# The merge stage of an attention plus mixture-of-experts layer: denser head storage, a two-tile projection with a bias row, and routing in five parts

## The reference

```
x = layernorm(x + (softmax(q k^T / 4 + gate * relative_bias) v) Wo^T + bo)
logits = x Wr^T ; probs = softmax(logits) ; best two of 8 experts, capacity 2560 rows each, in token order
token that overflows any expert -> a shared fallback net instead
x = layernorm(x + sum of expert outputs by weight)
```

## Time and profile before

| | us |
|---|---|
| median of 3 runs (lowest, highest) | 3783.45 (3782.28, 3784.93) |
| the profiled execution's own time | 3788.6 |
| its span | 3786.7 |
| `merge` in it, from its first transfer to the last scatter's issue | 2386.1 to 2675.9 |
| TensorE busy over the span | 3360.6 (89%) |
| mean granted TensorE clock | 0.94 |

### The profile page before, as it was taken

The page is one execution under the profiler, slowest core; times in us unless marked ns, Lnnn a source line. Parts: engine busy times, 40 slices in busy tenths (PEclk is TensorE's granted clock), DMA queues, the critical chain, the costliest instruction groups (busy, mean ns, idle before and its releaser), DMA issues. The chain is left out here.

```text
span 3786.7 us, 61590 instructions
## 1 busy us (share of the span) xinstructions
PE 3360.6 (89%) x20980; PEld 2171.0 (57%) x20980; DVE 2150.9 (57%) x5133; ACT 2131.6 (56%) x4135; POOL 1305.1 (34%) x1788
## 2 busy tenths in 40 slices
PE   7994998989999999999999898685599999999992
PEld 4552444444444444444444443574588888888882
DVE  5765887878787878787778786376011111111115
ACT  4553887878787878787878787111222232232231
POOL 3333433333333333333333332037323223222221
PEclk9997999999999999999999999896799999999996
DMA  6666233343434333333343432663465565665666
GB/s 196 218 223 145 52 67 75 66 81 67 78 67 76 68 80 69 79 66 75 75 78 64 75 66 49 176 205 137 161 204 191 190 205 188 193 204 186 196 196 202
DMA packets 281897, 481.68 MB, mean 127 GB/s; under 512 B 59906, under 2 KB 166020, under 8 KB 263170
## 3 DMA queue, kind: packets, MB, share of 16 engines
q1 hardware_dynamic: 243970, 425.27, 42.1%
q0 software_dynamic: 26880, 35.87, 4.5%
q10 hardware_dynamic: 10752, 16.78, 1.2%
HBM read 323.47 MB, written 153.89 MB: 126 GB/s over the span
## 5 line engine op out<-in xcount | busy, mean ns | idle before, releaser
L745 DVE CUSTOM_DVE_ANT_0 tot<-sc,gbias 128x1024 f32<-128x1024 f32 x1024 | 1238.8, 1210 | 34.1 <-PE sc L645 19.8
L612 POOL TENSOR_SCALAR gbias<-slab_a,gs 128x484 f32<-128x484 f32 x1024 | 679.7, 667 | 1099.2 <-DVE negm L745 826.1
L797 ACT ACTIVATE probs<-tot,negm 128x640 f32<-128x640 f32 (+2 forms) x1024 | 766.0, 748 | 83.9 <-DVE negm L745 81.7
L645 PE MATMUL sc<-ks,qs 120*128 120x512 bf16 x2048 | 638.5, 394 | 181.7 <-DMA gs<-gate_d 153.2
L1305 ACT ACTIVATE f_hid<-f_ph,f_w_up 128x256 f32<-128x256 f32 x576 | 272.7, 473 | 722.4 <-PE f_ph L1266 722.4
L806 ACT ACTIVATE far_t<-fb 128x512 f32<-128x512 f32 (+1 forms) x1024 | 580.2, 567 | 124.2 <-PE fb L682 116.7
L757 DVE COPY near_t<-pb 128x256 f32<-128x256 f32 (+1 forms) x1024 | 397.5, 388 | 373.2 <-PE pb L666 366.1
L816 ACT ACTIVATE near_t<-pa 128x256 f32<-128x256 f32 (+1 forms) x1024 | 447.8, 437 | 209.7 <-PE pa L657 197.0
L1266 PE MATMUL f_ph<-f_xt,f_w_up 128*128 128x256 f32 x2304 | 511.9, 380 | 5.7 <-DMA f_w_up<-in_w_up 5.0
L1278 PE MATMUL f_py<-f_w_down,f_hid 128*128 128x256 f32 x2304 | 509.0, 379 | 0.0
L657 PEld LDWEIGHTS pa<-ident,probs 128*128 128x128 f32 x2560 | 335.5, 144 | 253.5 <-issue 111.9
(11 more groups left out here) (164 smaller groups left out, 3092.9 us busy)
## 6 DMA issues: line engine op xcount, KB each, us to landing
f_w_down<-in_w_down SPq DMA_DIRECT2D x72, 1152.0 KB, 5.3
f_w_up<-in_w_up SPq DMA_DIRECT2D x72, 1028.0 KB, 7.7
xg_d<-fill SPq DMA_DIRECT2D x113, 260.0 KB, 5.2
ks<-k_d SPq DMA_DIRECT2D x192, 128.0 KB
qs<-q_d SPq DMA_DIRECT2D x192, 128.0 KB
f_xin<-xg_d SPq DMA_DIRECT2D x72, 260.0 KB, 5.2
v_d<-vt SPq DMA_DIRECT2D x16, 1024.0 KB, 6.2
vs<-v_d SPq DMA_DIRECT2D x32, 512.0 KB, 11.8
```

The source lines that it names most:

```text
L612: pool.tensor_scalar(gbias[x % NG][:, SIDE:SIDE + BAND], slab[:, hh, :], gs[u % 2][:, i, hh:hh + 1], 1.0, ALU.mult, ALU.mult).then_inc(gbi ...
L645: mm = pe.matmul(sc[:, x % 2, c * 512:(c + 1) * 512], qs[u % 2][0:120, hh, i * P:(i + 1) * P], ks[u % 2][0:120, hh, c * 512:(c + 1) * 512] ...
L745: dve.tensor_tensor_reduce(tot[x % 2][:], sc[:, x % 2, :], gbias[x % NG][:, w:w + N], -1.0, 3.0e38, ALU.add, ALU.min, negm[h % 2][:, c:c + ...
L797: act.activation(probs[x % 2][:, 0:hi - lo], tot[x % 2][:, lo:hi], ACT.Exp, bias=negm[h % 2][:, c:c + 1], scale=-1.0).then_inc(near_done, 1)
```

## The change

Six edits, all but the first in `merge`:

1. `ot_d` has two groups of 128 full rows in place of four of 128 with padding; `store` issues four transfers of 16 rows each, and the waits count 64 for each half.
2. `project_out` is one product of a row of ones with `b_o`, then two of 128 rows; `w_o` and `b_o` come in one transfer each, and POOL clears nothing but sets `eps`.
3. `load` moves half as many bytes of attention output.
4. The constants count on a semaphore of their own, `consts_in`, for which TensorE and VectorE wait at iteration 6; the second load is queued ahead of them.
5. The token numbers are loaded as a tile of 128 by 64 and copied to `x1s` by one VectorE instruction.
6. The parts are 15, 14, 13, 11 and 11 tiles, so routing begins at iterations 22, 36, 49, 60 and 71.

```diff
-    ot_d = dram("ot_d", [HQ, B, P, N], F32)
+    ot_d = dram("ot_d", [EC, B, P, N], F32)
...
-                    sp.wait_ge(ot_stored, h * 16)
+                    sp.wait_ge(ot_stored, h * 64)
...
-                sp.dma_start(ot_d[g, b, :, s * 512:(s + 1) * 512], rcb[:]).then_inc(ot_stored, 16)
+                for hh in range(4):
+                    row = (g % 2 * 4 + hh) * D
+                    sp.dma_start(ot_d[g // 2, b, row:row + D, s * 512:(s + 1) * 512], rcb[32 * hh:32 * hh + D, :]).then_inc(ot_stored, 16)
...
-PARTS = (20, 18, 15, 11)
+PARTS = (15, 14, 13, 11, 11)
...
-        w_o = sb("w_o", [P, HQ, E])
+        w_o = sb("w_o", [P, EC, E])
+        b_o = sb("b_o", [1, E])
-        otl = sb("otl", [P, NB, HQ, TC * P])
+        otl = sb("otl", [P, NB, EC, TC * P])
...
-            sp.wait_ge(w_zero, 1)
-            for h in range(4):
-                sp.dma_start(w_o[32 * h:32 * h + D], a["wo"].rearrange("(g h d) n -> h d g n", h=4, d=D)[h]).then_inc(loaded, 16)
-
-            sp.dma_start(w_o[D:D + 1, 0, :], a["bo"]).then_inc(loaded, 16)
+            sp.dma_start(w_o[:], a["wo"].rearrange("(c p) n -> p c n", p=P)).then_inc(loaded, 16)
+            sp.dma_start(b_o[:], a["bo"]).then_inc(loaded, 16)
+            load(1)
             with nc.allow_non_contiguous_dma(reason="small constants, once"):
                 for to, of in consts:
-                    sp.dma_start(to, of).then_inc(loaded, 16)
-            for c in range(1, NCH):
+                    sp.dma_start(to, of).then_inc(consts_in, 16)
+            for c in range(2, NCH):
                 load(c)
...
-            pool.memset(w_o[:], 0.0).then_inc(w_zero, 1)
-            pool.memset(eps[:], EPS).then_inc(w_zero, 1)
+            pool.memset(eps[:], EPS).then_inc(eps_set, 1)
...
-                for g in range(HQ):
-                    mm = pe.matmul(py[:, n % 3, 0:E], otl[:, c % NB, g, t * P:(t + 1) * P], w_o[:, g, :], start=g == 0, stop=g == HQ - 1)
+                pe.matmul(py[:, n % 3, 0:E], all1[0:1, :], b_o[:], start=True, stop=False)
+                for g in range(EC):
+                    mm = pe.matmul(py[:, n % 3, 0:E], otl[:, c % NB, g, t * P:(t + 1) * P], w_o[:, g, :], start=False, stop=g == EC - 1)
...
-            pe.wait_ge(loaded, 16 * LOADS)
+            pe.wait_ge(loaded, 16 * W_LOADS)
+            pe.wait_ge(ones_set, 1)
             for n in range(SLOTS_N):
+                if n == 6:
+                    pe.wait_ge(consts_in, 16 * len(consts))
...
-            dve.wait_ge(loaded, 16 * LOADS)
-            dve.memset(all1[:], 1.0)
+            dve.memset(all1[:], 1.0).then_inc(ones_set, 1)
...
+                if n == 6:
+                    dve.wait_ge(consts_in, 16 * len(consts))
+                    then(dve.tensor_scalar(before[:], before[:], 1.0, None, ALU.subtract))
+                    then(dve.tensor_copy(x1s[:, :, E + 3], token[:]))
```

More of the change, by code:

```diff
@@ L594, in _ @@
                                  fill[:].rearrange("p (o e) -> p o e", o=1).to_broadcast([P, FILL, 2 * XW])).then_inc(filled, 16)
-            sp.wait_ge(ot_stored, 16 * NH)
+            sp.wait_ge(ot_stored, 64 * NH)
         @block.gpsimd
@@ L891, in merge @@
         before = sb("before", [P, P])
+        token = sb("token", [P, TT])
         all1 = sb("all1", [P, P])
@@ L897, in merge @@
         pp = es.enter_context(nc.psum_tensor("m_pp", [P, 512], F32))
-        loaded, w_zero = sem("loaded"), sem("w_zero")
+        loaded, consts_in, eps_set, ones_set = sem("loaded"), sem("consts_in"), sem("eps_set"), sem("ones_set")
         in_ready = [sem(f"in_ready{k}") for k in range(NB)]
@@ L909, in merge @@
                   (first[:], a["c_first"]), (tile_n[:], a["c_tile"]), (level[:], a["c_level"]), (region[:], a["c_step"]),
-                  (x1s[:, :, E + 3], a["c_token"])]
-        LOADS = len(consts) + 5
+                  (token[:], a["c_token"])]
+        W_LOADS = 2
         def part_of(m):
@@ L1008, in _ @@
         def _(act):
-            act.wait_ge(w_zero, 2)
+            act.wait_ge(eps_set, 1)
             for n in range(SLOTS_N):
@@ L1162, in measure @@
                 dve.bn_aggr(mv[:, c % 2, t], stats[:, t]).then_inc(mean_done, 1)
-            dve.wait_ge(loaded, 16 * LOADS)
-            dve.memset(all1[:], 1.0)
+            dve.memset(all1[:], 1.0).then_inc(ones_set, 1)
             dve.memset(ones[:], 1.0)
             then(dve.memset(count[:], 0.0))
-            then(dve.tensor_scalar(before[:], before[:], 1.0, None, ALU.subtract))
             for n in range(SLOTS_N):
+                if n == 6:
+                    dve.wait_ge(consts_in, 16 * len(consts))
+                    then(dve.tensor_scalar(before[:], before[:], 1.0, None, ALU.subtract))
+                    then(dve.tensor_copy(x1s[:, :, E + 3], token[:]))
                 for q in range(len(PARTS)):
```

## The result

Before 3784.19 us (3782.28 to 3789.44, 4 runs), after 3877.7 (3874.73 to 3888.85, 4 runs): a ratio of 1.0249, 95% interval 1.0231 to 1.0267. The change makes the kernel 2.5% slower where 0.7% faster was forecast. The profiled execution has a span of 3872.9 us, against 3786.7.

A forecast was written before the change was run, and what follows sets the result against it. Merge was taken as bound by POOL's scatters, 1.28 us each, after part 1's routing. Earlier routing moved merge's end from 2675.9 to 2650.0 (-25.9), the profiled execution from 3788.6 to 3762.7; median 5.15 lower, 3757.5 us; range 3740 to 3773.

The forecast's parts named there:

- the clock stays down: Rival: in merge's routing steps TensorE falls to half clock, 4.9 us a step; up to +59 us, 3817; chance 0.10.
- the one-row product: Bias product in each tile's projection: taken at 0.41 us like 128 rows; if free, -8 us more.
- first projection after the opening: Start of merge: less data to load, so 7.8 us after the opening; -7.7 us (-8.1 to -4.7).
- routing begins after the opening: Tiles before routing in merge: fewer and shorter, so routing begins at 2438.0, 27.7 us sooner.
- part 0: Routing of the first part in merge: 35.4 us in place of 40.1, routed at 2473.4, 32.3 us sooner.
- first scatter: POOL's first scatter in merge: about 2474, some 33 us sooner.
- POOL idle between parts: POOL in merge: waits some 12 us in four gaps, since routing and not the scatters holds merge.
- last scatter after the opening: End of merge: 176.6 us after part 0 is routed, at 2650.0 against 2675.9.
- The 1.3 that I allowed: First two routing steps of part 0: 1.3 us less if a shorter opening brings the clock back sooner (0 to 2.9).
- the rival on them: Rival: three more store issues delay each unit's loads in attend; +30 to 40 us, 3790 to 3797; chance 0.04.
- the one on the opening: Rival: constants or weights still come last at merge's start; 7 us less gain, 3765; chance 0.04.
- the queue stays fed: Rival: POOL's scatters in merge end 164.6 us after part 0; 12 us more gain, or 3745; chance 0.12.

The follow-up runs named there:

- bias128: The changed kernel with the bias product over 128 rows (constant 1/128) instead of one: 3845.73 us, 0.9924 of before, on a chip with stops.
- row_and_full: The changed kernel with a third full product, of zeros, behind the one-row product in each tile: 3874.53 us, 1.0022 of before.
- bias128_again: The changed kernel with the bias product over 128 rows, run once more on a chip without stops: 3760.64 us, 0.9927 of before.
- before_row: The kernel before with a one-row product of zeros added ahead of each tile's four full products: 3948.48 us against 3873.46 before.
- after_warm: The changed kernel with 24 full products into an unused buffer ahead of the first tile: 3907.29 us, 1.0107 of before.
- nobias: The changed kernel with the bias product left out, so its output lacks the bias: 3847.14 us.

## Why the prediction was wrong

The step that failed is the one on which the rival "the clock stays down" was argued away: "at half clock TensorE would be busy without a pause, which is where the rows show the clock come back". On it the sum put all tiles but the first two, and all routing steps with a projection but a part's first one or two, at full clock. The rows showed it for tiles of eight full records. The changed tile was busy without a pause and the mean clock from 2380 to 2770 was 0.50. That the bias row is the cause is shown: `bias128` changes its rows alone and is 100 us faster, and `row_and_full` puts full work beside it and has the clock back. On the chips without stops, where the changed kernel took 3877.7 and `bias128_again` 3760.64, the single row costs 117 us. That activity releases the throttle (the Trainium skill, TensorE: Matmul & The Clock Gate, Part 1: The HAM clock gate) was taken as "this case mends itself". For such work this trace doesn't bear it out: busy 20.00 of 20 us, granted 0.50.

The rival itself was right in its mechanism and too small in its size. Its routing step of 4.9 us measured 5.10 (2493.71 less 2488.61). But its 59 us counted only the 27 steps with a projection. The clock had to be read for the free stretch too: 43.3 us are lost before the first routing, which the forecast put at full clock but for two tiles. I gave the rival 0.10, and all slower outcomes together 0.05.

The second failed term is the one-row product, "bounded by nothing and by a product of 128 rows (0.41 us)". It lay outside the bounds: in `before_row` it adds 0.7 us to a tile at full clock. The 0.41 was a row's price for 128 rows, and no row stood behind it as a bound for one. At full clock `after_warm` has a tile of 2.25 us (PE's timeline: 0.62 + 0.97 + 0.22 + 0.44) against 1.97 with 128 rows: 0.28 us more, of which 0.10 is the product and the rest shows in the work behind it. Of the 0.41 that a tile should have saved (2.40 to 1.99), 0.15 were left even at full clock. A rule used for it is that a weight load's time goes by columns and not rows (the Trainium skill, TensorE: Matmul & The Clock Gate, Step-by-step: what each phase is for). The loads' own durations agree nearly: in the changed kernel the median is 306 ns over one row (line 974) and 337 over 128 (line 976). But how long a load takes isn't when the next one may start, and there lay the cost.

The other steps are judged best on `bias128_again`, which has all of the change but the single row:

| step | forecast | `bias128_again` |
|---|---|---|
| first projection after the opening | 7.8 | 9.3 (8.1 in the changed kernel) |
| routing begins after the opening | 50.9 | 50.9 |
| part 0 | 35.4 | 36.8 |
| first scatter | about 2474 | 2474.26 |
| POOL idle between parts | 12 | 17.4 (6.11, 8.60, 2.23, 0.51) |
| last scatter after the opening | 262.9 | 268.5 |
| last scatter | 2650.0 | 2653.90 |
| ratio to before | 0.9931 | 0.9927 |
| median | 3757.5 | 3760.64 |

Part of the agreement is luck: `merge` opened at 2385.41, 1.7 us before the forecast, and hides as much of the 5.6 us by which it is longer. The first projection, released by the load of the bias, is later there; that its 128 rows are the reason was not tried apart. Part 0 is longer in its first two steps: they take 4.70 and 4.40 us, for which I had 10.1 - 1.6 - 1.3 = 7.2 in all. TensorE goes into them after a wait of 4.91 us, at half clock (a pair of records of `count_up` takes 0.43 us until the next, later 0.22). The 1.3 that I allowed for a clock that comes back sooner wasn't there. The stores cost nothing that shows in `attend` (SP still waits 662.7 us for POOL in that line, 670.7 before), as the queue's slack in the earlier trace rows said; the rival on them and the one on the opening fell. That the queue stays fed fell too: POOL waits in all four places.

So the change as a plan was sized rightly in its total, and one operand's shape reversed it. Not settled: why 64 rows came up late and 32 not in any window read, why the clock comes back with a one-row product in one routing and not in the next (`before_row`), and whether the clock follows the rows of the array that work or some sum over the products; nothing here looks inside. Also argued only: that `nobias` and `bias128` come to the same time because what one saves in work it loses in clock. Only float32 products with 128 columns of weights were tried.

## What to carry to other kernels

Read the granted clock beside the busy share: TensorE busy 100% of the time at 0.50 is not at its limit, and what it lacked here was full work, not less work. A rank-one product (a bias row) was dear in this float32 chain: spread it over 128 rows (here 100 us of 3946), or keep it in a padding row that is multiplied anyway, as the kernel before did. Adding it on another engine wasn't tried. And when a change takes full products out of a stretch that begins at half clock, price that stretch at both clocks before you price anything else; being warm and becoming warm are two questions.

## What was not expected of the hardware

- A product over 1 or 32 rows beside two full ones leaves the granted clock at 0.50 with TensorE busy 20.00 of 20 us; over 128 rows it rises to 1.00 in the free stretch.
- Even beside four full ones a one-row product can go with a clock of 0.50 in routing steps, with TensorE busy 55.00 of 55 us.
- The same tiles hold a clock of 1.00 for 45 us if they find it there.
- A weight load starts 0.65 us late next to a one-row product at half clock, whether that comes first or last, and behind one over 64 rows too; the one-row product takes 1.15 us, a full one 0.94.
- On some chips `merge` has stops of up to 32 us on several engines once the scatters have begun (65.4 us in six waits of ScalarE), and the kernel before takes 3866 to 3876 us instead of 3784. What stops them was not tried.
